# Shared expert B's transposed rows: from expert A's copy by way of DRAM, in place of transposes of its own

## The reference, cut to what matters

```
h  = layernorm(x) * (1 + cb) + sb            # 2048 x 512, "rows"
h1, h3 = h @ W1[e], h @ W3[e]                # 8 routed experts (top 2 of 8 per token), 512 x 352
y  = (silu(h1) * h3) @ W2[e]                 # 352 x 512
shared = (silu(h @ sw1.T) * (h @ sw3.T)) @ sw2.T    # 704 wide, every token
x  = x + gb * (sum of routed y * weight + shared)
```

## Time and profile before

| what | value |
|---|---|
| median of 3 executions | 567.3 us (567.28 to 568.34) |
| profiled execution: its own time | 568.31 us |
| profiled execution: span of the trace | 566.6 us |
| what lies around the span | 1.7 us |
| granted TensorE clock, mean | 0.994 |
| TensorE matmul busy | 545.8 us, 96% |
| VectorE / ScalarE / GpSimd busy | 53% / 32% / 46% |
| DMA | 107.19 MB, mean 189 GB/s |

### The profile page before, as it was taken

One profiled execution on the slowest core, in us unless ns is written; L12 is line 12 of the kernel. 1 busy time (PEld: TensorE's weight loads), 2 busy tenths in 40 slices (PEclk: granted clock), 3 DMA queues, 4 the chain that ended last, 5 costly groups with the idle time before them and its releaser, 6 DMA issues.

```text
span 566.6 us, 11166 instructions
## 1 busy us (share of the span) xinstructions
PE 545.8 (96%) x3184; PEld 490.3 (87%) x3185; DVE 301.5 (53%) x631; ACT 181.1 (32%) x347; POOL 263.2 (46%) x221
## 2 busy tenths in 40 slices
PE   8997799999999999999999999999999999999995
PEld 3666688988999999899999999999999999889994
DVE  3788776696677667632222222222222222479886
ACT  1444346345443442133222322232222322222210
POOL 2599886677667456443053430053535100245531
PEclk9998999999999999999999999999999999999998
DMA  8999245331332597566255754267676222367744
GB/s 306 395 330 333 75 153 219 131 111 74 111 122 103 175 331 292 185 225 223 95 185 203 278 183 178 90 215 267 214 259 206 91 74 74 112 208 221 225 157 137
DMA packets 41113, 107.19 MB, mean 189 GB/s; under 512 B 4224, under 2 KB 4224, under 8 KB 41088
## 3 DMA queue, kind: packets, MB, share of 16 engines
q1 hardware_dynamic: 28288, 54.44, 27.3%
q0 software_dynamic: 12800, 52.43, 26.8%
HBM read 76.19 MB, written 30.67 MB: 189 GB/s over the span
## 4 chain that ended last, share of the span: by engine, by line
PE 82%; POOL 6%; DVE 5%; issue 3%; DMA 2%; ACT 1%; SPq 0%; DVEq 0%; POOLq 0%
PE bank L946 15%; PE bank L947 14%; PE bank L948 14%; PE bank L962 8%; PE bank L960 8%; PE bank L961 8%; PE bank L929 5%; PE bank L967 4%; PE bank L898 2%; PE bank L900 2%; PE bank L899 2%; DMA x_all<-wmod 2%; POOL x_all L552 1%; POOL tmpa L544 1%; POOL tmpa L549 1%
## 5 line engine op out<-in xcount | busy, mean ns | idle before, releaser
L946 PE MATMUL bank<-whi,thi 128*128 (+1 forms) x416 | 139.0, 334 | 0.0
L947 PE MATMUL bank<-wlo,thi 128*128 (+1 forms) x416 | 134.6, 324 | 0.0
L948 PE MATMUL bank<-whi,tlo 128*128 (+1 forms) x416 | 134.3, 323 | 0.0
L536 POOL TENSOR_TENSOR wlo<-raw,whi 128x1408 f32 (+3 forms) x24 | 79.7, 3334 | 87.2 <-DMA whi<-w_all 75.0
L960 PE MATMUL bank<-whi,gth 128*128 (+1 forms) x204 | 80.9, 396 | 2.4 <-DVE gtl L1668 1.3
L962 PE MATMUL bank<-whi,gtl 128*128 (+1 forms) x204 | 80.6, 395 | 0.0
L961 PE MATMUL bank<-wlo,gth 128*128 (+1 forms) x204 | 79.9, 391 | 0.0
L1653 DVE TENSOR_TENSOR gbuf<-s,bank 128x352 f32<-128x352 f32 x52 | 27.1, 521 | 98.5 <-ACT s L873 97.6
L947 PEld LDWEIGHTS bank<-wlo,thi 128*128 128x128 f32 x416 | 78.5, 189 | 0.0
L946 PEld LDWEIGHTS bank<-whi,thi 128*128 128x128 f32 x416 | 78.5, 189 | 0.0
L948 PEld LDWEIGHTS bank<-whi,tlo 128*128 128x128 f32 x416 | 78.3, 188 | 0.0
(11 more groups left out here) (201 smaller groups left out, 970.3 us busy)
## 6 DMA issues: line engine op xcount, KB each, us to landing
raw<-w_all POOLq DMA_DIRECT2D x8, 2176.0 KB, 10.4
whi<-w_all POOLq DMA_DIRECT2D x16, 704.0 KB, 11.5
h<-xs_rows SPq DMA_DIRECT2D x36, 256.0 KB, 2.7
ys_rows<-tmpa SPq DMA_DIRECT2D x36, 256.0 KB, 2.0
x_all<-wmod SPq DMA_DIRECT2D x6, 1024.0 KB, 9.9
whi<-w_all POOLq DMA_DIRECT2D x8, 768.0 KB, 4.6
hs_rows<-h SPq DMA_DIRECT2D x8, 512.0 KB, 2.9
h<-hs_rows SPq DMA_DIRECT2D x16, 256.0 KB, 2.7
```

The lines of the kernel that those rows point to most:

```text
L536: pool.tensor_tensor(wlo[:, bass.ds(off + (SH + a), b - a)], raw[:, a:b], whi[:, bass.ds(off + (SH + a), b - a)].bitcast(F32), ALU.subtrac ...
L946: pe.matmul(dst, xh[:, j, a], wh, start=(m == 0), stop=False)
L947: pe.matmul(dst, xh[:, j, a], wl, start=False, stop=False)
L948: mm = pe.matmul(dst, xl[:, j, a], wh, start=False, stop=(m == KD - 1))
```

## The change

Expert A's transposed parts of each pair are stored to two DRAM tensors, and expert B loads them straight into `xbh` and `xbl`. B's own 16 turns on TensorE, 16 `high` on ScalarE and 16 `lows` on VectorE go; section S keeps them. ScalarE's `high_a` now also waits for the stores of the pair before. The buffer of two tiles is refilled when the `up` that reads it is done. `early` goes. Cut to the core (the counts of section S that lose their offset, and the same edit on other engines, are left out):

```diff
+    xth = nc.dram_tensor("xt_high", (T, D), F32, kind="Internal").ap()
+    xtl = nc.dram_tensor("xt_low", (T, D), F32, kind="Internal").ap()
+        def routed_next(i, j, c, sec):
+            if sec == "B":
+                return i * 2 + j == NB - 1
+            return sec == "S" and not (c == -1 and j == 1)
...
+            def load_x(t, j):
+                for dst, src in ((xbh, xth), (xbl, xtl)):
+                    sp.dma_start(dst[:, j, :].bitcast(F32), src[t * P:(t + 1) * P, :]).then_inc(q["C", "xin"][j], 16)
+            def store_x(p):
+                sp.wait_ge(q["A", "xlo"], p * 2 + 2)
+                for dst, src in ((xth, xah), (xtl, xal)):
+                    sp.dma_start(dst[bass.ds(p * 2 * P, 2 * P), :].rearrange("(b p) d -> p b d", p=P),
+                                 src[:, :, :].bitcast(F32)).then_inc(s_xts, 16)
             def body(it, lo, hi):
                 if lo == NP + 2:
+                    sp.wait_ge(s_stp, NP)
+                    sp.wait_ge(s_xts, 32 * (NP - 1))
+                    for t in range(2):
+                        load_x(t, t)
                     sp.wait_ge(s_nat, NP * 16)
-                    sp.wait_ge(s_h2T, NP)
-                    for t in range(2):
-                        load(hs, t, t * P)
                     sp.wait_ge(s_xd, NP)
                     rows_of_pair(NP - 2, 1)
                     sp.wait_ge(s_scat, 64 * (NP - 2))
                     rows_of_pair(NP - 1, 0)
...
+                if live(3, lo, hi):
+                    store_x(it - 3)
                 if live(2, lo, hi):
...
             for t in range(2, NB):
-                sp.wait_ge(q["S", "xt"], t - 1)
-                load(hs, t % 2, t * P)
+                sp.wait_ge(q["S", "up"], t - 1)
+                load_x(t, t % 2)
+            sp.wait_ge(s_xts, 32 * NP)
+            sp.wait_ge(s_h2T, NP)
...
+            def next_c(k):
+                if k < NT - NB:
+                    sp.wait_ge(q["S", "up"], iters * 2 + (NB + k - 1))
+                    load_x(NB + k, k % 2)
...
             def high_a(p, lo):
                 act.wait_ge(s_h2T, p + 1)
                 if lo > 3:
                     act.wait_ge(q["A", "up"], p * 2)
+                    act.wait_ge(s_xts, p * 32)
...
             def up(...):                                   # TensorE
+                if loaded is not None:
+                    pe.wait_ge(q["C", "xin"][j], loaded * 32)
...
                 if lo == NP + 2:
                     ranks(it - 4)
-                    turn(0, 0, bank[6])
...
             def step(i, j, c, sec):
...
-                if not last and not early:
-                    next_turn()
+                if routed_next(i, j, c, sec):
+                    pe.wait_ge(q["A", "y"], NT)
+                    if sec == "S" and not (isinstance(i, int) and i + j == CB):
+                        pe.wait_ge(q["S", "xlo"], (i - CB) * 2 + j)
                     turn(i + j, 1 - j, bank[j])
```

More of the change, by code:

```diff
@@ L239, in build @@
         s_h2T = sem("s_h2T")
+        s_xts = sem("s_xts")
         s_lg = sem("s_lg")
@@ L322, in steps @@
                     step(i, j, None, "S")
-            with eng.Fori(CB + 2, iters + CB) as i:
+            with eng.Fori(CB + 2, iters + (CB - 1)) as i:
                 for j in range(2):
                     step(i, j, None, "S")
+            for j in range(2):
+                step(iters + (CB - 1), j, -1, "S")
             first = NP - 1 if unrolled else CB + 2
@@ L424, in next_b @@
                 row = row_of(s * 2 + (j + 3))
-                sp.wait_ge(q["S", "xt"], s * 2 + (j + 2 + NB))
+                sp.wait_ge(q["S", "xt"], s * 2 + (j + 2))
                 load(xs, 1 - j, row)
-            def next_c(s, j, tile):
-                sp.wait_ge(q["S", "xt"], s * 2 + (j + 2 + NB))
-                load(hs, 1 - j, tile * P)
+            def next_c(k):
+                if k < NT - NB:
+                    sp.wait_ge(q["S", "up"], iters * 2 + (NB + k - 1))
+                    load_x(NB + k, k % 2)
             def row_of(n):
@@ L455, in _ @@
                 row = row_of(n)
-                sp.wait_ge(q["S", "xt"], NB - 1 + n)
+                if n > 1:
+                    sp.wait_ge(q["S", "xt"], n - 1)
                 load(xs, n % 2, row)
@@ L468, in _ @@
             store_y(iters - 3, 1)
[L469 to L472, removed]
+            store_y(iters - 2, 0)
+            for j in range(2):
+                next_c(j)
+                store_y(iters + (j - 2), 1 - j)
             for c in range(CB, NP):
                 for j in range(2):
-                    if 2 * c + j + 3 < NT:
-                        next_c(iters + (c - CB), j, 2 * c + j + 3)
-                    if c + j == CB:
+                    k = (c - CB) * 2 + j
+                    next_c(k + 2)
+                    if k == 0:
                         store_y(iters - 1, 1)
-                    elif 2 * c + j + 3 < NT:
+                    elif k < NT - NB - 3:
                         store_out(c - 1 + j, 1 - j)
@@ L598, in body @@
                     for t in range(2):
-                        pool.wait_ge(q["S", "xin"][t], 16)
+                        pool.wait_ge(q["C", "xin"][t], 32)
                     fetch_raw(0)
@@ L858, in step @@
                 first, last = sec == "B" and i + j == 0, sec == "C" and isinstance(c, int) and c * 2 + j == NT - 1
[L859 to L863, removed]
+                if routed_next(i, j, c, sec):
+                    act.wait_ge(q["S", "up"], i * 2 + j)
                     high(i + j, 1 - j, bank[j])
-                if not last and not early:
-                    next_high()
                 act.wait_ge(q["S", "up"], i * 2 + (j + 1))
@@ L930, in transposes, with up @@
                 return mm
-            def up(sec, i, j, off, there=None):
+            def up(sec, i, j, off, there=None, loaded=None):
                 xh, xl = (xah, xal) if sec == "A" else (xbh, xbl)
-                pe.wait_ge(q[sec, "xlo"], i * 2 + (j + 1))
+                if loaded is not None:
+                    pe.wait_ge(q["C", "xin"][j], loaded * 32)
+                elif sec == "A":
+                    pe.wait_ge(q["A", "xlo"], i * 2 + (j + 1))
+                else:
+                    pe.wait_ge(q["S", "xlo"], (i - CB) * 2 + (j + 1))
                 for m in range(KD):
@@ L970, in turn @@
             def turn(i, j, dst):
-                pe.wait_ge(q["S", "xin"][j], i * 16 + 16)
+                pe.wait_ge(q["S", "xin"][j], (i - CB) * 16 + 16)
                 transposes(dst, xin[:, j, :]).then_inc(q["S", "xt"], 1)
@@ L1126, in step @@
                 first, last = sec == "B" and i + j == 0, sec == "C" and isinstance(c, int) and c * 2 + j == NT - 1
-                early = sec == "B" and i == 0
                 off, before = WSZ, WSZ
@@ L1148, in step @@
                     pe.wait_ge(q["S", "g"], i * 2 + j)
-                up("S", i, j, off, [NW + 1, NW + 2] if sec == "B" else need_up)
+                up("S", i, j, off, [NW + 1, NW + 2] if sec == "B" else need_up,
+                   i + 1 if sec == "B" else c + 1 if sec == "C" else None)
                 if first:
                     ranks(NP - 1)
-                if early:
-                    next_turn()
-                if first:
                     last_tile(NP - 1, NP + 3)
@@ L1629, in step @@
                 first, last = sec == "B" and i + j == 0, sec == "C" and c * 2 + j == NT - 1
[L1630 to L1634, removed]
+                if routed_next(i, j, c, sec):
+                    dve.wait_ge(q["S", "up"], i * 2 + j)
                     lows(i + j, 1 - j, bank[j])
-                if not last and not early:
-                    next_lows()
                 if sec == "B" and i * 2 + j == 1:
```

10 lines of the change are left out of this document (2 added, 8 removed).

## The result

| | kernel before | kernel after |
|---|---|---|
| median, us | 567.70 (567.28 to 568.70, 7 runs) | 572.96 (570.24 to 574.93, 7 runs) |
| profiled execution, us | 568.31, span 566.6 | 573.36, span 571.7 |

The account below looks back on a forecast made before the run. TensorE was taken as the bound, its matmuls busy 96% of the span. +0.2 + 3.9 + 0 - 3.5 = +0.6 us gave 568.9 for the profiled execution, 567.9 for the median; 8-in-10 range 564.0 to 571.2.

Parts of the forecast that it names:

- The turn's worth: Each turn removed from TensorE was to save 0.38 to 0.39 us; 16 turns, 6.2 us at most.
- End of stage A: Pair 6's stores hold xah 0.5 to 1.1 us late against 1.0 us of reserve; +0.2 us taken.
- Section B as TensorE alone sees it: Turns of B0 to B3 go, 1.56 us; VectorE's gbuf in B1 limits the gain to -1.4 us.
- Section B as the DMA queues see it: 1.57 MB more in saturated queues moves the last scatter and R0's turn from 225.9 to 229.8: +3.9 us replacing -1.4.
- signs of failure: The prediction fails if R0's turn comes before 227 or after 232, or TensorE waits for loads in section C.
- the queue starves B2's load: Rival, 31%: B2's load, behind 1.05 MB of stores, lands later than about 224; at the bound +3.8 us, 571.1.
- my half: In section B each queue gets half, 0.20 MB/us, once scatters follow the weights; B2's load lands at 222.5.
- Section S: Keeps its turns; its stall at the first routed step moves with B3's turn_g; 0 us.
- Section C: 12 turns go; gathers and VectorE set the pace early, larger loads beside gathers may delay: -3.5 us (3.1 to 3.7).

Follow-up runs that it names:

- e2: The kernel after with only pair 7's two stores moved behind the loads of B2 and B3; 569.44 us, ratio 1.0028 to before.
- e5: e1 with B2's and B3's parts loaded early, at about 194 us, into spare buffers; 566.01 us, ratio 0.9953 to before.
- e8: e7 with pair 7's two stores moved behind the loads of R0's and R1's rows; 564.40 us, ratio 0.9913 to before.
- e3: The kernel after with six matmuls of zeros on TensorE ahead of B2's up; 570.40 us, ratio 1.0039 to before.
- e9: The kernel after run once more, unchanged; 571.64 us, ratio 1.0050 to before.
- e1: The kernel after with each pair's stores issued before the row load, pair 7's at about 194 us; 567.43 us, ratio 0.9993 to before.
- e4: The kernel after without the loads of C4 and C5; 569.50 us, ratio 1.0030 to before.
- e12: e8 run again, unchanged, on the chip of e11; 561.12 us, ratio 0.9879 to before.
- e11: e8 without the one-step shift of the finish of tiles 0 to 3 in section C; 563.26 us, ratio 0.9922 to before.
- e10: The kernel after with only the finish of tiles 0 to 3 in section C shifted one step later; 572.93 us, ratio 1.0047 to before.
- e6: e5 with the finish of tiles 0 to 3 in section C one step later; 570.10 us, ratio 1.0018 to before.
- e7: e6 with the last shifted output store placed between the outputs of C9 and C10; 567.17 us, ratio 0.9967 to before.

## Why the prediction was wrong

**The turn's worth, 0.38 to 0.39 us: right.** The late step is 6.30 us, and the stretch from C4 on gave 2.38 against the 2.3 forecast.

**End of stage A, +0.2: too small, 1.46.** The store landed 5.92 us after its issue, at 191.5, or 192.1 on before's clock (after's execution is 0.63 us ahead); I had 190.4 to 191, and 1.0 us of reserve. The mechanism and the place were named and the stated bound was 1.0. In after it did not reach the end, as I read it (no run shows it alone): B2's load lands when it lands, and a TensorE that is later at B2 waits that much less there. It counts in a kernel where B2 doesn't wait, as e2, where the same step took 7.07 us, 0.57 over before.

**Section B as TensorE alone sees it, -1.4: right.** The steps of B0, B1 and B2's turn give 0.98 in after; where nothing is waited for (e5, e8), B2's turn_g, the last milestone before R0's turn, comes 1.39 us earlier than in before from the same start.

**Section B as the DMA queues see it, +3.9: the step that failed.** Its first half held in size. R0's rows were issued at 226.49 instead of 223.22, and with the 0.63 us that after's execution was ahead, that is 3.9 us later, the forecast to the tenth. The closeness is in part luck: in e3 and e9, with the same order of DMAs, they are 3.2 and 3.7 us later, and in e1, with as many bytes but the stores earlier, 2.0. What failed is the other half: "B2's 0.52 MB at 220.6, and with 2 us of fixed part it lands at 222.5 ... a wait of about 4 us ... TensorE is at R0's turn at 228.5, before R0's rows". The load was there at 224.4, or 225.0 on before's clock, 2.5 us later than I had it, and from there to R0's turn it took 233.49 - 224.38 = 9.1 us, not 6.0. Of these 3.1 us, 2.7 are the `up` at the lower clock (6.69 us instead of 3.98). The other 0.4 is a slip: the 6.4 us of the earlier trace rows from the start of B2's `up` to R0's turn hold no turn (B3's lies in front of that `up`), so nothing was to be taken off them. So R0's turn came at 234.1 on before's clock, not at 228.5, and the rows, which I had as the later of the two, were no longer waited for. Of the 5.6 us between, 2.5 are the landing, 2.7 the clock after it and 0.4 the turn; the prediction gave a wait its length as its price and nothing for what comes behind. Its own signs of failure came true: R0's turn after 232, a wait of 5.1 us at B2 instead of about 4, and none at R0's turn instead of 1. The rival "the queue starves B2's load" had the right place and mechanism; its bound of 571.1 was too low by that same missing term. On its landing: by the Trainium skill's "DMA: Bandwidth & Descriptors", section on queues, rings and completion order, the prediction had worked out 226 with a third of the packets' bytes for SyncE's queue, and 222.5 with my half. The trace says 225.0 (224.2 in e3, 224.7 in e9, from the same start): later than my half gives in all three, and in after nearer to the page's rule.

**Section S, 0: nearly.** B3's to R0's turn_g takes 7.46 us instead of 7.82, here and in e1, e5, e8 and e9, a gain of 0.36 that I had not forecast and that no run explains. The rest of the 2.25 from B3 to C2 is four turns and 0.4 at C2's wait.

**Section C, -3.5: -2.4.** The late part is right. The start isn't: "0 to 0.6" for larger loads beside the gathers was 2.3 us (after against e4; 1.4 to 2.8 over the other executions with these loads). The sum had looked at the transfers on SyncE's queue and whether they were in time for `up`, which they were; it had not asked what a gather on GpSimd's queue loses to them.

The sum, then: -0.6 (start of the execution) + 1.5 + 6.6 - 2.4 = +5.1, against +0.2 + 3.9 - 3.5. The miss of 4.5 us is 2.7 (the clock after B2's wait) + 0.4 (the turn taken off) + 2.5 (the landing) - 1.3 (by which R0's rows had been forecast behind TensorE) at the entry to section S, + 1.1 in section C, - 0.3 (the 0.2 of stage A, which I take as swallowed by B2's wait, and 0.1 in B3's step) and - 0.6 (the start).

**Open.** Why TensorE's signal reaches ScalarE late in seven of the traces is not shown, only that these are the seven that lack records; e8 has it and its exact repeat e12, on another chip, has not. Each kernel has one profiled execution, so how often it comes is not known. What decides how much is lost after a wait of TensorE (1.3 to 2.7 us behind B2's, see e3) is open too. Whether B2's landing follows packets or bytes was not separated either.

## What to carry to other kernels

Before a transpose is replaced by a trip through DRAM, look up when the DMA engines are full, and put stores that nobody waits for behind the loads that TensorE waits for; here the order of stores and loads in one queue, with two spare buffers for early loads, decided between 1.005 to 1.008 (after, e9) and 0.992 (e11) with nearly the same instructions. Price a wait of TensorE by its length and by the work that follows at the lower clock: here 1.1 to 2.7 us more behind waits of 2.9 to 5.1 us, and nothing behind waits of 0.2 to 2.3 us. And a load that is in time for its own reader can still make another queue's gather late.

## What the runs showed of the hardware

After TensorE had stood for 5.11 us, the granted clock was 0.50 in 224 to 228 and 0.69 in 228 to 232: an `up` of 3.98 us took 6.69. After waits of 4.5 to 4.8 us it took 5.2 to 5.7 (e4, e9, e10), after 2.9 and 3.2 us 5.5 and 5.1 (e1, where the clock was 0.57 in 228 to 232, and e2), after 1.0 to 2.3 us 4.0 (e5, e6, e7, e11). With matmuls of zeros in the wait it took 4.04 at a clock of 1.00 (e3). Not expected either: a 5.92 us landing for a 0.52 MB store behind 1 MB, where loads of that size had a median of 3.7. A gather of 0.26 MB took 4.2 us with C4's and C5's loads left out (e4) and 5.6 to 7.0 with them (after 6.5). And in seven traces, all of which lack semaphore records, the semaphore of TensorE's turn_g in C3 was raised 2.8 to 3.5 us after the turn_g had ended.
